# Mixture of experts rewritten without a loop as eighteen steps over five runs of one tile shape each, on a static ring of four banks

## What is computed

```python
h = relu(x @ sW1 + sb1); h = relu(h @ sW2 + sb2); shared = h @ sW3 + sb3
gates = softmax(x @ gW + gb)             # 4 experts
top, idx = top_k(gates, 2); w = softmax(top)
h = relu(einsum('baf,efh->ebah', x, eW1) + eb1)
h = relu(einsum('ebah,ehg->ebag', h, eW2) + eb2)
o = einsum('ebag,ego->ebao', h, eW3) + eb3
y = x + shared + sum over the chosen of w * o
```

## Time and profile before

| | us |
|---|---|
| median of three runs | 1000.75 |
| lowest and highest | 1000.44, 1000.97 |
| the profiled execution's own time | 999.74 |
| its span, first to last instruction | 997.9 |
| busy in it: TensorE / VectorE / ScalarE / GpSimd | 937.3 / 743.0 / 501.4 / 435.9 |
| mean granted clock of TensorE | 0.988 |

### The profile page before, as it was taken

How to read it: one execution, slowest core, us unless ns; L and a number is a source line. 1 busy time by engine, 2 the same in 40 slices (tenths; PEclk the granted TensorE clock), 3 DMA queues, 4 the chain that set the end, 5 groups by cost and what they waited for, 6 DMA issues and landing times.

```text
span 997.9 us, 24586 instructions
## 1 busy us (share of the span) xinstructions
PE 937.3 (94%) x9608; PEld 368.2 (37%) x9608; DVE 743.0 (74%) x1261; ACT 501.4 (50%) x799; POOL 435.9 (44%) x259
## 2 busy tenths in 40 slices
PE   3799999999999999999999989996999999999996
PEld 1234344343433434334343433222333333333332
DVE  4687887878878788787887858995676666666664
ACT  3555454554545545454454412446655655646643
POOL 3677676776767767677676510000101001001000
PEclk9999999999999999999999999997999999999998
DMA  9468778787887878878788450000000000000000
GB/s 376 115 185 243 251 224 258 215 243 247 226 264 210 244 242 229 265 209 243 240 233 270 122 140 2 0 1 0 1 19 13 11 21 11 11 21 11 11 22 22
DMA packets 64150, 141.46 MB, mean 142 GB/s; under 512 B 22592, under 2 KB 22592, under 8 KB 55872
## 3 DMA queue, kind: packets, MB, share of 16 engines
q1 hardware_dynamic: 64064, 140.18, 48.2%
HBM read 68.85 MB, written 4.19 MB: 73 GB/s over the span
## 4 chain that ended last, share of the span: by engine, by line
PE 83%; DVE 10%; issue 2%; DMA 1%; POOL 1%; ACT 1%; SPq 0%; DVEq 0%; POOLq 0%
PE ring L801 21%; PE bank_ms L773 11%; PE qp L838 11%; PE bank_sq L773 6%; PE ring L994 5%; DVE sb_prodv L1166 4%; PE ring L1005 4%; PE bank_ms L1035 3%; PE qp L972 2%; PE bank_sq L994 2%; PE ring L988 2%; PE ring L935 2%; PE bank_ms L1005 2%; PE bank_ms L1027 2%; PE bank_sq L1014 1%
## 5 line engine op out<-in xcount | busy, mean ns | idle before, releaser
L801 PE MATMUL ring<-sb_arena,sb_wqkv 64*64 64x512 f32 x2048 | 266.3, 602 | 19.9 <-DVE sb_prodv L1166 17.6
L1166 DVE TENSOR_TENSOR sb_prodv<-ring,sb_wbc 128x1024 f32<-128x1024 f32 x128 | 154.0, 1206 | 32.7 <-PE ring L801 30.2
L1135 DVE TENSOR_TENSOR sb_prodk<-ring,sb_qbuf 128x1024 f32<-128x1024 f32 x128 | 153.3, 1220 | 18.1 <-PE ring L801 15.5
L537 POOL TENSOR_TENSOR sb_parts_q<-sb_arena,sb_const 128x512 fp32r<-128x512 f32 x15 | 15.6, 1039 | 305.8 <-ACT sb_arena L657 305.8
L406 POOL TENSOR_TENSOR sb_rows<-sb_arena 128x2048 f32<-128x2048 f32 x31 | 141.5, 4564 | 16.7 <-DMA sb_arena<-x 16.6
L838 PEld LDWEIGHTS qp<-sb_prodv,sb_tok_w 64*64 64x64 f32 x4096 | 119.6, 133 | 54.7 <-issue 51.4
L838 PE MATMUL qp<-sb_prodv,sb_tok_w 64*64 64x128 f32 x4096 | 128.4, 269 | 2.5 <-DVE sb_prodv L1166 2.5
L580 ACT ACTIVATE sb_xsq<-sb_arena 128x2048 f32<-128x2048 f32 x64 | 118.4, 1896 | 10.0 <-DMA sb_arena<-x 10.0
L801 PEld LDWEIGHTS ring<-sb_arena,sb_wqkv 64*64 64x64 f32 x2048 | 58.5, 131 | 153.4 <-issue 81.8
L503 POOL TENSOR_TENSOR sb_score<-sb_score,sb_smx 128x512 f32<-128x512 f32 x32 | 40.9, 1277 | 82.3 <-DVE sb_smx L1149 82.3
L408 POOL TENSOR_TENSOR sb_rows<-sb_rows 128x1024 f32<-128x1024 f32 x31 | 74.0, 2386 | 2.4
(11 more groups left out here) (202 smaller groups left out, 1480.4 us busy)
## 6 DMA issues: line engine op xcount, KB each, us to landing
sb_arena<-x SPq DMA_DIRECT2D x64, 1024.0 KB, 8.6
sb_wbc<-sb_wgt SPq DMA_DIRECT2D x256, 256.0 KB, 5.7
out<-sb_arena SPq DMA_DIRECT2D x64, 64.0 KB, 1.9
sb_rest_w<-rest_w SPq DMA_DIRECT2D x1, 918.5 KB, 22.6
sb_const<-const SPq DMA_DIRECT2D x1, 264.5 KB, 3.0
sb_tok_w<-tok_w SPq DMA_DIRECT2D x1, 260.5 KB, 2.9
sb_const<-const SPq DMA_DIRECT2D x1, 256.0 KB, 22.6
```

Of the source, the lines that this page charges most:

```text
L801: mm = pe.matmul(ring[slot][C * half:C * half + C, i, :], image_block(w, i), x[C * i:C * i + C, m, half, c], start=True, stop=True)
L1135: dve.tensor_tensor(by_pixel(prodk[:, c]), by_pixel(ring[c % 2][:, :, :]), q[:, :, None, :].to_broadcast([P, 2, N_PIX, G32]), ALU.mult).th ...
L1166: dve.tensor_tensor(prodv[:, :, :, G32 * c:G32 * (c + 1)], by_pixel(ring[k % 2][:, :, :]), by_pixel(wbc[:, c]), ALU.mult).then_inc(values_ ...
```

## The change

The hardware loop is gone; all engines run through `range(ITERS + 2)` written out, 18 steps, and a step of TensorE holds work of three iterations, ordered so that matmuls of one tile shape stand together. Iteration i's first and second layers are in step i; its spread routing weights, biases and third layers in step i+1; its output rows in step i+2. The centred rows, variance and logits of iteration i+1 are in step i.

The ring has four banks; the sum has the fifth, `bank_sum`, to itself, with the semaphores `sum_mm` and `sum_taken`. A dictionary `slots`, filled when the kernel is built, numbers the 19 uses of a step in order, and use s takes bank s mod 4. The expert biases now open the sum and the shared third layer comes after them. The routing weights are turned into `bank_base` instead of `bank_var`. `h2` has three buffers instead of two, `h2s` four instead of two.

The relus are shared out by use, no longer by bank: VectorE does one of each pair of first expert layers (four) and one of the shared second layer, ScalarE the other five, the shared first layer and the four second expert layers. On VectorE `gates` now ends before the ranks, which are a function of their own, and comes ahead of all its relus.

```diff
-        mix_ring = banks[0:3] + banks[6:8]
+        bank_sum = banks[7]
+        mix_ring = banks[0:3] + banks[6:7]
...
+        slots = {}
+        def book(*use):
+            slots[use] = len(slots)
+        for i in range(ITERS + 1):
+            if i < ITERS:
+                book("shared1", i)
+                for e in range(E):
+                    for m in range(2):
+                        book("expert1", i, e, m)
+                for m in range(2):
+                    book("shared2", i, m)
+            if i >= 1:
+                for n in range(4):
+                    book("spread", i - 1, n)
+            if i < ITERS:
+                for n in range(4):
+                    book("expert2", i, n)
...
+            def claim(*use):
+                pe.wait_ge(taken[slots[use] % RING], slots[use] // RING)
+                return bank_of(*use)
...
             def out_rows(i):
-                pe.wait_ge(taken[K_SUM % RING], USES // RING * i + K_SUM // RING + 1)
+                pe.wait_ge(sum_taken, i + 1)
                 pe.wait_ge(out_ready, i)
+                pe.wait_ge(routing_low, min(i + 2, ITERS))
...
+            for i in range(ITERS + 2):
+                live, ahead, late = i < ITERS, i + 1 < ITERS, 1 <= i <= ITERS
+                if live:
+                    shared_first(i)
+                if ahead:
+                    centre_rows(i + 1)
+                if live:
+                    turn_logits(i)
+                if i >= 2:
+                    out_rows(i - 2)
+                if live:
+                    experts_first(i)
+                    shared_second(i)
+                if late:
+                    spread_routes(i - 1)
+                if ahead:
+                    variance(i + 1)
+                if live:
+                    experts_second(i)
+                if late:
+                    third_layers(i - 1)
+                if ahead:
+                    logits(i + 1)
+                if live:
+                    turn_routing(i)
```

`spread_routes` is the four spreads and then the two float32r bias matmuls that open the sum; `third_layers` the shared and the expert third layers. ScalarE and VectorE:

```diff
+            for i in range(ITERS + 2):
+                live, ahead, behind = i < ITERS, i + 1 < ITERS, i >= 2
+                if live:
...
+                    act.activation(lg_rows, bank_var[:, 0:P], ACT.Copy).then_inc(logits_copied, 1)
+                    relu_shared1(act, i)
+                if ahead:
+                    norm_sq(i + 1)
+                if live:
...
+                    act.activation(lgx, lgx, ACT.Exp).then_inc(logits_exp, 1)
+                if behind:
+                    out_sq(i - 2)
+                if live:
+                    relu_expert1(act, i, 0, 0)
+                    relu_expert1(act, i, 1, 0)
...
+                    act.activation(pick, pick, ACT.Exp).then_inc(gates_exp, 1)
+                    relu_expert1(act, i, 2, 0)
+                    relu_expert1(act, i, 3, 0)
+                    relu_shared2(act, i, 0)
+                if behind:
+                    out_rstd(i - 2)
+                if ahead:
+                    norm_rstd(i + 1)
+                if live:
+                    for n in range(4):
+                        relu_expert2(act, i, n)
...
-                routing(i)
-                relu(dve, i, 2)
-                gates(i)
-                relu(dve, i, 7)
-                chosen(i)
-                if prev:
-                    square_sum(i - 1)
-                if not isinstance(i, int) or i + 1 < ITERS:
-                    normed(i + 1, (p + 1) % 2)
-                relu(dve, i, 12)
-                route_low(i)
-                if prev:
-                    finish(i - 1, (p + 1) % 2)
-                for n in range(4):
-                    weigh(i, n)
-                total(i, p)
+            for i in range(ITERS + 2):
+                live, ahead, late, behind = i < ITERS, i + 1 < ITERS, 1 <= i <= ITERS, i >= 2
+                if live:
+                    routing(i)
+                    gates(i)
+                    for e in range(E):
+                        relu_expert1(dve, i, e, 1)
+                    relu_shared2(dve, i, 1)
+                if behind:
+                    square_sum(i - 2)
+                if late:
+                    for n in range(4):
+                        weigh(i - 1, n)
+                if behind:
+                    finish(i - 2, i % 2)
+                if live:
+                    ranks(i)
+                    chosen(i)
+                if ahead:
+                    normed(i + 1)
+                if late:
+                    total(i - 1)
+                if live:
+                    route_low(i)
```

More of the change, by code:

```diff
@@ L992, in mstep @@
                     for m in range(2):
                         rows = slice(C * m, C * m + C)
-                        pe.matmul(pair[m][:, :], ew1[rows, e, :], h2[rows, p, :], start=True, stop=True).then_inc(ring_mm, 1)
-                    if e == 0 and prev:
-                        out_rows(i - 1)
-                if nxt:
-                    variance(i + 1)
-                for k in range(9, K_SHARED):
-                    im, q = (k - 9) % 2, (k - 9) // 2
-                    bank = ring_use(i, k)
+                        pe.matmul(pair[m][:, :], ew1[rows, e, :], h2[rows, i % 3, :], start=True, stop=True).then_inc(ring_mm, 1)
@@ new lines, in shared_second, with spread_routes @@
+            def shared_second(i):
+                wait_taken(pe, "shared1", i)
+                pair = [claim("shared2", i, m) for m in range(2)]
+                for m in range(2):
+                    rows = slice(C * m, C * m + C)
+                    pe.matmul(pair[m][:, :], sw2[rows, :], h1s[rows, :], start=True, stop=True).then_inc(ring_mm, 1)
+            def spread_routes(i):
+                pe.wait_ge(routing_low, i + 1)
+                for n in range(4):
+                    pe.matmul(claim("spread", i, n)[:, :], exact[0:N_ROUTE, H_SEL + n * P:H_SEL + (n + 1) * P],
+                              route[0:N_ROUTE, :], start=True, stop=True).then_inc(ring_mm, 1)
+                pe.wait_ge(sum_taken, i)
+                pe.matmul(bank_sum[:, :], exact[0:N_ROUTE, H_B3:H_SEL], route[0:N_ROUTE, :], start=True, stop=False,
+                          skip_group_check=True)
+                pe.matmul(bank_sum[:, :], b3_low[0:N_ROUTE, :], route[0:N_ROUTE, :], start=False, stop=False,
+                          skip_group_check=True)
@@ L1007, in mstep @@
                     mm.then_inc(ring_mm, 1)
-                    if k == 11:
-                        turn_routing(i, nxt)
-                pe.wait_ge(taken[0], USES // RING * i + 1)
-                pair = [ring_use(i, K_SHARED + m) for m in range(2)]
-                for m in range(2):
-                    rows = slice(C * m, C * m + C)
-                    pe.matmul(pair[m][:, :], sw2[rows, :], h1s[rows, :], start=True, stop=True).then_inc(ring_mm, 1)
-                if not isinstance(i, int) or i + 2 < ITERS:
-                    centre_rows(i + 2)
```

205 lines of the change are left out of this document (80 added, 125 removed).

## The result

The changed kernel takes **1008.24 us** (median of 5 runs, 1006.31 to 1013.98) against 1000.73 for the kernel before in the same comparison (997.86 to 1000.97). The ratio is 1.0091 with a 95% interval of 1.0067 to 1.0114: 0.9% slower. The profiled execution took 1007.29 us, with a span of 1005.3.

A forecast was written before the change was run, and what follows sets the result against it. TensorE's order of work was taken to bound the kernel: 18.48 - 1.75 - 0.28 = 16.45 us a step, plus waits, taken as 18.77. Span 988.0 + 8.0 + 9.4 = 1005.4, on the median 1008 us; range 991 to 1014.

The forecast's parts named there:

- Shapes: TensorE's matmuls: five runs of one tile shape a step instead of fifteen, saving 1.75 us of shape entries.
- Rival (e): TensorE: 40-row matmuls are another shape than 64x128; 0.19 us more a step, 1011 us; chance counted within the forecast's 0.49.
- the table: One step laid out from the last routing transposition of the step before, engine by engine: 18.77 us.
- The hold: VectorE's gates: GpSimd's splits hold small operations, delaying the relu that frees a bank; third pair waits 1.31 us, plus 0.08.
- Rival (a): VectorE's gates slip through without being held by GpSimd's first split: step 17.7, about 993 us; chance 0.20.
- The ring's other waits: Four-bank ring: TensorE waits 0.26 + 0.08 us before the shared second layer and 0.54 before the third spread.
- rival c: Second expert layers: VectorE 0.6 us later than laid out, TensorE waits 0.3 more a step, 1012.5 us; chance 0.13.
- The ends: Step 0, step 15 and the work after it: 988.0 + 8.0 + 9.4 = 1005.4 us, 3.5 us of the growth.
- 4 in the steps: Steps 1 to 14, all taken as 18.77 us, 0.29 more than before: 4 us of the span's 7.5 us growth.

The follow-up runs named there:

- late split: Changed kernel, with GpSimd's first split starting only when the gates' last subtraction is done: 995.26 us, ratio 0.9956 to the kernel before.
- late split and the biases between: Changed kernel with the late split, and the two bias matmuls between the second and third spread: 988.94 us, ratio 0.9892 to the kernel before.
- outputs inside: Changed kernel with the eight output matmuls between the experts' first and second pair: 1009.15 us, ratio 1.0087 to the kernel before.

## Why the prediction was right, and where it was not

The time (1008 against 1008.24) and the span (1005.4 against 1005.3) came out closer than the working deserves: two errors of nearly 2 us cancelled, which is luck. By its steps:

**Shapes: right.** Five runs a step, 0.43 us a pass in the long run, and the 40-row matmuls go with 64x128: the first spread comes 1.01 us after the shared second layer's first pass (846.72 to 847.73), where two passes, the 0.08 of their weights and an entry of 0.20 would make 1.14; with the late split and the biases between it comes after 0.74 us. Rival (e) is out. One entry stands elsewhere than counted: the turned routing (L1054, tiles of 128 rows by 8 columns) goes into the shape of the shared first layer, which starts right behind it, and the entry lies ahead of both: from the logits to the shared layer it is 0.80 us (856.60 to 857.40), where the table leaves 0.60 and puts 0.20 behind. The shared layer then takes 0.86 us for two passes; the table had it at 0.20 and centring at 1.17, 0.97 apart. This is the 0.11 us by which the step (18.66) is shorter than foretold (18.77).

**The hold: right, its size within 0.2 us.** Both splits hold a gate operation, L537 (now L566) too, whose case rested on a farther row. From the first pair's start, the table said 3.13 us to the third pair, 5.19 to the shared second layer, 7.14 to the third spread, 8.83 to the second layers; the rows above give 2.97, 5.11, 7.04 and 8.83. The first three are early because GpSimd's first split started 0.27 us ahead of the first pair, and not 0.11; by the second layers nothing of it is left. In the sum the wait of the third pair was 1.31 + 0.08; by starts the hole is 1.15. That the hold is the cause was read from two ends that coincide; the late split and the changed kernel without a split now show it, 0.79 us a step, and the kernel before without one shows that it cost nothing there. The prediction drew on the Trainium skill, "SBUF — State Buffer", SBUF: two separate sides, for the lock; these runs agree with it: the operation that comes second waits, whether it is 0.07 us (L1396) or 0.90 (L1400) of waiting.

**Rival (a)** had nearly the right price. It gave a step of 17.7 and 993 us if the gates slipped through; with the late split, where they do, the step is 17.86 and the time 995.26.

**The ring's other waits: right in place, and the third spread over-sized.** 0.54 us was foretold between the spreads. By starts the hole is 848.65 - 848.04 - 0.24 = 0.37, and 0.45 a step came back when it was filled.

**VectorE's weighing (rival c): not seen**, in no plain step, not even at 17.40. The margin of 0.3 us held.

**The ends: right.** Step 0's last transposition ended at 708.2 (foretold 708.3), step 15's at 988.1 (988.0), the last sum started at 995.9 (996.0), and from there to the end it was 9.4 us. Against the kernel before, up to 1 us of the first interval is the clock's (see above), which no term of the sum held. The ends are nearly half of the loss: -4.3 for the first interval, +0.65 for the last and +7.0 behind it make 3.4 of the 7.4 us, the prediction's 3.5.

**What was wrong: "4 in the steps".** It was 13 x 0.16 = 2.1 in the plain steps, since the step was 0.11 shorter than foretold, and 1.9 in one long step, 0.35 for a late relu and 1.6 for a stretch of half clock, of which the prediction says nothing. It took all steps for equal and the clock for full throughout them, as before's trace has it. In the five runs of the changed kernel the longer span goes with the lower mean clock: 1004.1 us at 0.989, 1005.3 and 1006.1 at 0.987, 1008.0 at 0.986, 1011.8 at 0.982. One stretch makes 0.0017 of the mean clock (half the clock for 3.4 of 1005 us) and costs 1.6 us, 0.9 us for each 0.001; 7.7 us come with 0.007 between the shortest run and the longest. So a few such stretches more in the long runs, four or five by this estimate, are the likely reading. It is not shown, since one of the five runs alone has a trace, and what sets a stretch off stays open.

Also not tried: five banks for the ring beside the sum's own, since all eight are taken (three with fixed jobs, the sum's, the ring's four); and another order of the last, half-empty steps, where TensorE waits 1.50 us for the low part of the routing.

## What to carry to other kernels

Removing work from the bounding engine helps only if the engines that hand it its buffers can keep the new pace: here some 1.8 us of shape changes came off each step, by the prediction's reckoning, and a ring shortened by one bank gave them back, with one relu queued behind five small operations, one of them held by GpSimd. Before moving an operation on a queue, ask what buffer the operations behind it free; what was harmless there before (a small VectorE operation held by GpSimd) sits on the path afterwards. And work that needs no buffer of the ring belongs where the ring is late: moving two matmuls by two places was worth 0.45 us a step.

## What was not expected of the hardware

- A matmul with tiles of 128 rows by 8 columns shares its shape with 128x128 here: no entry between L1054 and L1000 (four transpositions in 0.43 us from 856.97, then two passes in 0.86 from 857.40).
- A VectorE operation of 32 elements a partition is held for as long as GpSimd's operation lasts, and ends some 0.05 us behind it in each of the 15 steps that have the splits: 1.09 us instead of 0.19. One that meets only the last part of GpSimd's (L1396) is held only for that, 0.26 us.
- TensorE, 92% busy in its plain steps and with holes of about 1 us, was granted half the clock for some 3.4 us of one step at 924 us, which cost 1.6 us. The same came at the same place in three variants, and in a fourth (outputs inside) at another, 715 us.
- An entry into a shape (0.2 us) costs nothing inside a wait: two of them left a step at 18.65 as it was, and at 17.84 against 17.86; at 17.48 against 17.40 some of it shows.
